# Zero fills moved behind the second pair's loads, and four cross-attention pieces moved within steps 4 and 5, in a one-core decoder layer

## The chip, the cores and the metric

One core of a Trainium2 chip runs the whole kernel as one launch. The metric is the device time of one execution in microseconds (us). The engines are TensorE (PE), VectorE (DVE), ScalarE (ACT), GpSimd (POOL) and SyncE (SP); SP computes nothing here and issues most of the DMAs.

## The reference, cut to what matters

A pre-norm decoder layer for 8 sequences of 100 tokens and width 512: self attention (16 heads, 4 key-value heads, rotary), cross attention to a context of 345 + 16 rows, and a feed-forward part with a shared expert and 60 routed experts, of which each token takes 4. The context's last 16 rows ("DCA") have their own keys, values and softmax.

```python
x = x + attn(layernorm(x))                     # self attention
q = ln(layernorm(x) @ Wq + bq)
ctx     = softmax(q @ k.T * s) @ v             # 345 context rows
ctx_dca = softmax(q @ k_dca.T * s) @ v_dca     # the 16 DCA rows
x = x + (ctx + ctx_dca) @ Wo + bo
x = x + shared(layernorm(x)) + sum_of_top4_experts(layernorm(x))
```

## The kernel before, in words

Each engine has an instruction list of its own, written out by hand, and the lists meet at semaphores. The attention part runs as a loop over 4 pairs of sequences (`i` = 0 to 3; `j` = 0, 1 is the sequence in a pair). Then the routed experts run, two tiles at a time, with the shared expert beside them.

**A pair.** PE begins with the transposes of the normed input (`transpose_x("xT1", 1, j)`), ACT copies them into `xT[j]` (lines 1410 to 1412), and PE projects q, k and v from there (`self_project`). Self attention follows, then the cross attention in steps `t` = 0 to 9. Step `t` takes four of the 32 (sequence, head) combinations: PE computes their scores (`four_scores(t)`), DVE the maxima (`four_max`), ACT the exponentials, PE transposes the previous four (`four_transposes(t - 1, c)`), DVE copies these out (`four_T`), and PE multiplies the ones before with the values (`four_values(t - 2)`). `keep_busy` puts in products of zeros. In the gaps DVE works at the layer norm of the next pair's x, a few instructions at a time (`norm_next`, `few(n)`); it waits for that x (`x_loaded`).

**PSUM.** The eight banks are handed out by a list that `attention_fills` builds from the same hooks that PE's list uses. `HEAD_HOOKS[t]` are PE's extra pieces ahead of a step's transposes, `STEP_HOOKS[t]` those after the first two of them, `TAIL_HOOKS[t]` those after the third. A piece begins only when the earlier user of its bank has been read out. The DCA scores of the second sequence, `("ds", 1)`, and the spread sums of the first, `("rx", 0)`, lie one after the other in bank 7.

**DCA and the sums.** `dca_scores(j)` puts the DCA scores into PSUM; `dca_softmax(j)` on DVE is a generator of three parts: maximum and subtraction (lines 1818 and 1819, which free the bank), sum, reciprocal. `sums(j)` takes the reciprocal of the sums of the main softmax (line 1830) and scales the DCA probabilities (lines 1831 and 1832). ACT spreads the reciprocals over 512 columns (`spread_sums`, `t0`), PE transposes them (`spread_T`, "rx"); from the scaled probabilities PE makes `dca_transpose`, "dpT". In the kernel before, `sums(0)` stands at the end of DVE's step 4, behind the last `few`, and the first part of `dca1` behind it.

**SP's list.** At the start come the weights, then `load_context(1, 0)`, then nine fills of zeros (line 473): 76 tiles of `xs_d` and 36 tiles of `ys_d`, 128 rows of 2 KB each, at most 13 tiles a DMA. Only the scatter and the gather of the routed experts need them. Then, pair by pair: `load_x(i + 1)` (line 433), `load_context(i + 1, 1)` (line 436, once PE has made the values `("vx", 1, 2)` in step 0), and at the pair's end the stores of `xT[0]` into `xT3_d` (line 523), of `xn` and of `xr` (lines 529 and 530). `xT[0]` then holds the transposed input of the gate; ACT overwrites it at the next pair's begin, and for that it waits for the store:

```python
act.wait_ge(xT_stored[0], i * 16 + 1)     # line 1410
x_T("xT1", 0)
x_T("xT1", 1)
```

POOL normalises the heads of the cross attention's keys and queries (`head_norm`, lines 711 to 728), beside DVE's work in steps 1 to 7.

Of the kernel before, what the change touches and what calls it, by code (L numbers as in the profile page):

```python
# [38 lines left out]
TILES = SINGLES + ROUNDS  # L39
assert SINGLES == ROUNDS  # L40
NOV = 36
FILL_STEP = 13
ZERO_FILLS = -(-(TILES + NOV) // FILL_STEP) + -(-NOV // FILL_STEP)
# [39 lines left out]
def attention_fills():  # L83
# [17 lines left out]
    for t in range(STEPS):  # L101
# [4 lines left out]
        if t == 0:  # L106
            out += [(("vx", 1, 2), 7), (("kx", 0, 0), 4), (("xT2", 1), 5)]
        out += [(key, 7) for key in HEAD_HOOKS.get(t, [])]
        parts = [(("xpT", t - 1, c), 4 + (t * LN_ + c) % 2) for c in range(LN_)] if 1 <= t <= FOURS else []
        out += parts[:2] + [(key, 7 if t < 6 else 6) for key in STEP_HOOKS.get(t, [])] + parts[2:]  # L110
        out += TAIL_HOOKS.get(t, [])
# [2 lines left out]

HEAD_HOOKS = {5: [("rx", 0)]}
STEP_HOOKS = {1: [("xq", 1)], 2: [("kx", 0, 1)], 4: [("ds", 1)], 5: [("dpT", 0)], 6: [("xo", 0)], 7: [("vx", 0, 1)]}
TAIL_HOOKS = {3: [(("xqT", 1), 7), (("kx", 0, 2), 4)], 5: [(("vx", 0, 0), 7)], 8: [(("dpT", 1), 3), (("vx", 0, 2), 2)]}
STEP_ZEROS = {1: (0, 0), 2: (0, 2), 3: (3, 0), 4: (0, 2), 5: (2, 0), 6: (0, 2), 7: (0, 2), 8: (2, 0)}  # L120

# [1 line left out]
def decoder_kernel(nc, x, ctxT, dcaT, W_attn, W_out, b_out, Wq, bq, Wkv, bkv, Wdca, bdca, norm, Wo, bo,  # L123
# [6 lines left out]
    with cm:  # L130
# [3 lines left out]
        def sem(name):  # L134
            return cm.enter_context(nc.semaphore(name))
# [6 lines left out]
        xs_d = nc.dram_tensor("xs_d", [(TILES + NOV) * T, D], F32, kind="Internal").ap()  # L142
        ys_d = nc.dram_tensor("ys_d", [(TILES + NOV) * T, D], F32, kind="Internal").ap()
# [72 lines left out]
        vx = [carve(LN_, D) for _ in range(2)]  # L216
# [8 lines left out]
        dpT = [carve(2, S) for _ in range(2)]  # L225
# [87 lines left out]
        pool_pre = sem("pool_preamble")  # L313
# [108 lines left out]
        def wait_drained(eng, i, *key):  # L422

            k = bank_of[key]
            eng.wait_ge(free[k].sem, free[k].at(i, key))
# [3 lines left out]
        def _(sp):  # L429
# [5 lines left out]
            def load_context(i, j):  # L435
                sp.dma_start(c_in[j], ctxT[i * 2 + j, :, :, :]).then_inc(c_loaded[j], 16)
# [29 lines left out]
            sp.wait_ge(first_full, 2 * LN_)  # L466
            load_context(1, 0)

            sp.wait_ge(pool_pre, 7)
            def fill_zeros(rows, first, last):  # L470
                for n in range(first, last, FILL_STEP):
                    m = min(FILL_STEP, last - n)
                    sp.dma_start(rows[n * T:(n + m) * T, :].rearrange("(a p) d -> p a d", p=T),  # L473
                                 zero[0:T, :].rearrange("p (a d) -> p a d", a=1).to_broadcast([T, m, D])).then_inc(zeroed, 16)
                return -(-(last - first) // FILL_STEP)

            fills_started = fill_zeros(xs_d, 0, TILES + NOV)

            fills_started += fill_zeros(ys_d, TILES, TILES + NOV)
            assert fills_started == ZERO_FILLS  # L480

            def load_up(m):
                if m >= 3:
# [11 lines left out]
            for i in range(PAIRS):  # L495
                if i:
                    wait_drained(sp, i, "xT3", 1)
                    store_last_T(i - 1)

                if i:  # L500
                    sp.wait_ge(full[2].sem, full[2].before(i))
                    load_context(min(i + 1, PAIRS - 1), 0)

                sp.wait_ge(x1_ready, i * 2 + 2)
                sp.wait_ge(xr_ready.sem, xr_ready.at(i, (0, 1)))
                load_x(min(i + 1, PAIRS - 1))
                if i + 1 < PAIRS:

                    sp.wait_ge(full[7].sem, full[7].at(i, ("vx", 1, LN_ - 1)))
                    load_context(i + 1, 1)  # L510
                else:

                    sp.wait_ge(full[1].sem, full[1].at(i, ("o", 1)))
                    for j in range(2):
                        sp.wait_ge(xT_stored[j], 16 * i + 1)
                    load_tokens(0, 2 * i, xT3_early)
                    for m in range(3):
                        load_up(m)
                for j in range(2):
                    sp.wait_ge(xn_ready.sem, xn_ready.at(i, (3, j)))  # L520
                    if j == 0:
                        wait_drained(sp, i, "xT3", 0)
                        sp.dma_start(xT3_d[i * 2, :, :], xT[0].rearrange("p a b -> p (a b)")).then_inc(xT_stored[0], 16)
                    elif i == PAIRS - 1:
                        sp.wait_ge(xT_stored[0], 16 * PAIRS + 1)
                        load_tokens(2 * i, 2 * i + 1, xT3_loaded)
                        sp.wait_ge(late_free, 1)
                        store_last_T(i)
                    sp.dma_start(xn3_d[i * 2 + j, :, :], xn[j][0:S, :]).then_inc(xn_stored[j], 16)
                    sp.dma_start(x2_d[i * 2 + j, :, :], xr[j][0:S, :]).then_inc(x2_stored[j], 16)  # L530
# [259 lines left out]
        def _(pe):  # L790
# [30 lines left out]
            with pe.Fori(0, PAIRS) as i:  # L821
# [270 lines left out]
                for t in range(STEPS):  # L1092
# [11 lines left out]
                    if t >= 2:  # L1104
                        four_values(t - 2)
                    for key in HEAD_HOOKS.get(t, []):
                        hooks[key[0]](*key[1:])
                    if 1 <= t <= FOURS:
                        four_transposes(t - 1, 0)
                        four_transposes(t - 1, 1)  # L1110
                    for key in STEP_HOOKS.get(t, []):
                        hooks[key[0]](*key[1:])
# [460 lines left out]
        def _(dve):  # L1573
# [13 lines left out]
            def link(ins):  # L1587

                settle(mark(ins))
# [120 lines left out]
            with dve.Fori(0, PAIRS) as i:  # L1710
# [115 lines left out]
                def sums(j):  # L1826

                    for r in range(4):
                        wait_drained(dve, i, "xs", 4 * j + 3, r)
                    nc.vector.reciprocal(xrec[0:S, j, :], xsum[0:S, j, :]).then_inc(xrec_ready.sem, 1)  # L1830
                    link(nc.vector.tensor_tensor(drec[0:S, j, :], drec[0:S, j, :], xsum[0:S, j, :], ALU.mult))
                    nc.vector.tensor_tensor(dp[j][0:S], dp[j][0:S],
                                            drec[0:S, j, :].rearrange("p (a b) -> p a b", b=1).to_broadcast([S, H, DCA]),
                                            ALU.mult).then_inc(dp_ready.sem, 1)

                def four_max(t, r):
                    j, h = t // 4, 4 * (t % 4) + r
                    k = filled("xs", t, r)
                    nc.vector.tensor_reduce(xnm[0:S, j, h:h + 1], ps[0:S, k, 0:LM], AX, ALU.max, negate=True).then_inc(xmax_ready.sem, 1)  # L1839

                def four_T(t, c):
                    k = filled("xpT", t, c)
                    nc.vector.tensor_copy(xpT[0:LC, c, :], ps[0:LC, k, 0:4 * S]).then_inc(free[k].sem, 1)  # L1843
# [37 lines left out]
                dca0, dca1 = dca_softmax(0), dca_softmax(1)  # L1881
# [18 lines left out]
                def few(n):  # L1900
                    for _ in range(n):
                        next(pieces, None)
                for t in range(1, FOURS + 1):
                    if t == FOURS:
                        sums(1)
                        four_T(t - 1, 0)
                        four_T(t - 1, 2)
                        context_value(0, 2)
                        break
                    four_max(t, 0)  # L1910
                    four_max(t, 1)
                    if t == 6:
                        context_T(0)
                    if t == 7:
                        residual("xo", 0)
                    few(1)
                    four_max(t, 2)
                    four_T(t - 1, 0)
                    four_max(t, 3)
                    if t == 7:  # L1920
                        run(pieces)
                        dve.wait_ge(x1_ready, i * 2 + 4)
                        pieces = norm_x(0)
                    few(2)
                    four_T(t - 1, 1)
                    for key in STEP_HOOKS.get(t, []):
                        if key[0] in ("kx", "vx"):
                            (context_key if key[0] == "kx" else context_value)(*key[1:])
                        elif key[0] == "xq":
                            query(1)  # L1930
                    few(2)
                    four_T(t - 1, 2)
                    for key, _ in TAIL_HOOKS.get(t, []):
                        if key[0] in ("kx", "vx"):
                            (context_key if key[0] == "kx" else context_value)(*key[1:])
                    few(2)
                    if t == 4:
                        sums(0)
                        next(dca1, None)
                    if t in (6, 7):  # L1940
                        next(dca1, None)
                run(pieces)
# [248 lines left out]
```

## Time and profile before

| | us |
|---|---|
| median of 3 runs | 1183.49 |
| lowest, highest | 1182.42, 1189.03 |
| the profiled execution, its own time | 1185.29 |
| span of the profiled execution | 1183.3 |

PE is busy for 1096.6 us of the span (93%), DVE for 505.8, POOL for 371.5, ACT for 263.7. PE's time is the frame: a loss is where PE waits, or where its granted clock is low. Times are counted from the start of the span. A row of a timeline has start, duration, engine, line and tile, and in brackets how long the engine had been idle before it and what ended that. In a table of stretches the last three columns are PE's granted clock (1.00 is 2.4 GHz, 0.50 is 1.2 GHz), the share of the DMA engines and GB/s.

### The profile page before, as it was taken

What the parts mean: (1) busy time and instruction counts of PE and PEld (TensorE: products, weight loads), DVE (VectorE), ACT (ScalarE), POOL (GpSimd) and SP (SyncE); (2) the same over time, 40 slices, a digit from 0 to 9 for tenths busy, and PEclk for the clock granted to TensorE, in tenths of its full rate; (3) what the DMA queues carried; (4) which work ended last, traced back from release to release, by engine and by line L of the source; (5) the groups of instructions that cost most, each with busy time, mean ns of one, the idle gap of its engine ahead of it and who ended that gap; (6) DMA issues with size and microseconds to landing.
All of it is one profiled execution on the core that took longest, in us unless ns stands there. A gap on an engine that the chain in (4) does not pass through costs nothing.

```text
span 1183.3 us, 18962 instructions
## 1 busy us (share of the span) xinstructions
PE 1096.6 (93%) x5550; PEld 592.1 (50%) x5550; DVE 505.8 (43%) x1385; ACT 263.7 (22%) x806; POOL 371.5 (31%) x843
## 2 busy tenths in 40 slices
PE   3999799998999989999999999999999989899797
PEld 1444455445654455544655554555555544444454
DVE  7843574339654395544856701222122211211054
ACT  0332232424332242333414010111111110101000
POOL 2575451855427563474200271000000000000173
PEclk9999899999899999999999999999999998989999
DMA  8999301000010000102004896999999999999744
GB/s 307 325 398 383 114 3 56 15 1 13 2 56 15 13 2 11 46 15 96 1 28 121 306 341 224 384 371 371 379 366 375 368 380 362 376 374 376 252 132 128
DMA packets 76589, 233.17 MB, mean 197 GB/s; under 512 B 11362, under 2 KB 13766, under 8 KB 68814
## 3 DMA queue, kind: packets, MB, share of 16 engines
q1 hardware_dynamic: 58830, 197.90, 46.7%
q10 hardware_dynamic: 11520, 20.98, 5.1%
q0 software_dynamic: 6144, 13.13, 3.6%
q8 instruction: 47, 0.77, 0.3%
q14 instruction: 48, 0.39, 0.1%
HBM read 178.75 MB, written 53.22 MB: 196 GB/s over the span
## 4 chain that ended last, share of the span: by engine, by line
PE 60%; SPq 16%; DVE 10%; DMA 7%; issue 5%; ACT 1%; DVEq 0%; ACTq 0%
PE ps L851 14%; PE ps L935 7%; PE ps L1136 6%; SPq L473 6%; PE ps L1219 5%; PE ps L1320 5%; SPq L546 4%; PE ps L1215 4%; DMA arena<-in_w 3%; DMA arena<-in_se_down 2%; PE ps L1251 2%; PE ps L1247 2%; PE ps L992 2%; PE ps L1193 2%; SPq L551 2%
## 5 line engine op out<-in xcount | busy, mean ns | idle before, releaser
L851 PE MATMUL ps<-arena 128*100 128x512 f32 (+3 forms) x576 | 220.5, 529 | 5.2 <-ACT arena L1342 3.7
L785 POOL DMA_INDIRECT arena<-ys_d,slot_u x32 | 37.5, 1173 | 415.7 <-issue 413.8
L851 PEld LDWEIGHTS ps<-arena 128*100 128x100 f32 (+1 forms) x576 | 87.0, 173 | 100.3 <-issue 90.3
L1219 PE MATMUL ps<-arena 128*64 128x352 f32 x640 | 108.8, 497 | 15.3 <-DMA arena<-in_w 9.0
L2068 DVE COPY arena<-ps 128x512 f32<-128x512 f32 x40 | 27.7, 691 | 221.5 <-PE ps L1207 221.5
L935 PE MATMUL ps<-arena 128*100 128x512 f32 x256 | 114.1, 593 | 0.0
L1136 PE MATMUL ps<-arena 128*128 128x400 f32 x288 | 98.3, 501 | 2.3 <-DVE arena L2048 1.1
L1215 PE MATMUL ps<-arena 128*128 128x352 f32 x320 | 98.1, 459 | 0.8 <-issue 0.8
L1394 ACT ACTIVATE arena<-ps,arena 100x345 f32<-100x345 f32 x128 | 69.4, 546 | 112.4 <-DVE arena L1839 109.8
L1219 PEld LDWEIGHTS ps<-arena 128*64 128x64 f32 x640 | 49.9, 147 | 69.2 <-issue 61.5
L711 POOL TENSOR_TENSOR arena<-arena 115x512 f32<-115x512 f32 (+1 forms) x29 | 30.5, 1052 | 162.2 <-DVE arena L1766 125.0
L1136 PEld LDWEIGHTS ps<-arena 128*128 128x128 f32 x288 | 54.2, 190 | 44.9 <-DVE arena L1810 1.7
L1215 PEld LDWEIGHTS ps<-arena 128*128 128x128 f32 x320 | 59.2, 190 | 30.7 <-issue 1.0
L935 PEld LDWEIGHTS ps<-arena 128*100 128x100 f32 x256 | 42.3, 166 | 62.2 <-issue 58.8
L1508 ACT ACTIVATE arena<-ps 128x352 f32<-128x352 f32 x40 | 18.5, 463 | 223.9 <-PE ps L1219 130.3
L773 POOL DMA_INDIRECT xs_d<-arena,slot_u x32 | 32.6, 1020 | 109.1 <-DVE slot_u L2029 99.6
L1839 DVE TENSOR_REDUCE arena<-ps 100x1 f32<-100x345 f32 x128 | 62.3, 508 | 8.1 <-PE ps L983 7.6
L1320 PE MATMUL ps<-arena 128*128 128x400 f32 x176 | 61.1, 509 | 4.8 <-DMA arena<-in_se_down 4.8
L992 PE MATMUL ps<-ident,arena 100*115 100x100 f32 x384 | 55.4, 284 | 9.8 <-DVE arena L1843 9.1
L992 PEld LDWEIGHTS ps<-ident,arena 100*115 100x115 f32 x384 | 49.2, 193 | 26.3 <-DVE arena L1843 13.1
L1843 DVE COPY arena<-ps 115x400 f32<-115x400 f32 x92 | 52.2, 568 | 21.4 <-PE ps L992 21.3
L1251 PE MATMUL ps<-arena 128*64 128x512 f32 (+1 forms) x240 | 56.0, 600 | 1.0 <-DVE arena L2084 0.9
(227 smaller groups left out, 1522.5 us busy)
## 6 DMA issues: line engine op xcount, KB each, us to landing
arena<-in_w SPq DMA_DIRECT2D x60, 1408.0 KB, 16.8
arena<-in_w SPq DMA_DIRECT2D x60, 512.0 KB, 17.2
xs_d<-zero SPq DMA_DIRECT2D x5, 3328.0 KB, 25.4
arena<-in_w SPq DMA_DIRECT2D x60, 192.0 KB, 19.4
arena<-xs_d ACTq DMA_DIRECT2D x40, 256.0 KB, 8.3
ys_d<-arena ACTq DMA_DIRECT2D x40, 256.0 KB, 8.9
ys_d<-zero SPq DMA_DIRECT2D x2, 3328.0 KB, 25.7
arena<-in_se_up SPq DMA_DIRECT2D x11, 512.0 KB, 6.5
```

What stands on the lines that cost most here:

```text
L473: sp.dma_start(rows[n * T:(n + m) * T, :].rearrange("(a p) d -> p a d", p=T), zero[0:T, :].rearrange("p (a d) -> p a d", a=1).to_broadcast ...
L851: last = nc.tensor.matmul(ps[0:m, k, 0:cols[1] - cols[0]], lhs(c), w[:, c, cols[0]:cols[1]], start=(c == 0), stop=(c == n_c - 1))
L935: last = nc.tensor.matmul(ps[0:S, j, :], cT[c % 2][:, g, :], w_out[:, c * G + g, :], start=(c == 0 and g == 0), stop=(c == KV - 1 and g == ...
L992: last = nc.tensor.transpose(ps[0:LC, k, r * S:(r + 1) * S], xp[(4 * t + r) % NP_][0:S, c * LC:(c + 1) * LC], ident[0:S, 0:S])
L1136: last = nc.tensor.matmul(ps[:, (u % 3) * 2 + gu, 0:400].rearrange("p (a b) -> p a b", a=4), se_w[m % 3][:, c, gu * P:(gu + 1) * P], tok, ...
L1215: last = nc.tensor.matmul(ps[:, 1 + gu, 0:I], xsT[0][:, c, :], w13_s[s][0][:, c, at:at + I], start=(c == 0), stop=(c == DC - 1))
L1219: last = nc.tensor.matmul(ps[half * HALF:(half + 1) * HALF, 3 + gu, 0:I], xsT[1][:, c, half * HALF:(half + 1) * HALF], w13_s[s][1 + half][ ...
L1251: last = nc.tensor.matmul(ps[half * HALF:(half + 1) * HALF, 7, :], hT[1][0:w, n, half * HALF:(half + 1) * HALF], w2_s[s][1 + half][0:w, n, :],
L1320: last = nc.tensor.matmul(ps[:, half * 4 + d, 0:400], w_down[:, m, d * P:(d + 1) * P], hT_all[:, m, half * 400:(half + 1) * 400], start=(m ...
L1394: nc.scalar.activation(xp[(4 * t + r) % NP_][0:S, :], ps[0:S, k, 0:LM], ACT.Exp, bias=xnm[0:S, j, h:h + 1], scale=1.0, accum_out=xsum[0:S, ...
L1839: nc.vector.tensor_reduce(xnm[0:S, j, h:h + 1], ps[0:S, k, 0:LM], AX, ALU.max, negate=True).then_inc(xmax_ready.sem, 1)
L1843: nc.vector.tensor_copy(xpT[0:LC, c, :], ps[0:LC, k, 0:4 * S]).then_inc(free[k].sem, 1)
```

## The change

The nine fills of zeros are issued by SP within the first pair, after `load_x(1)` and `load_context(1, 1)`, and no longer ahead of them. The wait for the tile of zeros moves with them. In steps 4 and 5: PE computes `("ds", 1)` ahead of step 4's transposes and no longer after the first two of them; DVE takes the first part of `dca1` after the fourth maximum of step 4; `sums` is cut in two, the reciprocal (now after the second copy of step 4) and `scale_dca` (for sequence 0 after the second maximum of step 5). Two of the layer-norm pieces of step 4 move behind its third copy. For sequence 1 both halves stay together.

```diff
-HEAD_HOOKS = {5: [("rx", 0)]}
-STEP_HOOKS = {1: [("xq", 1)], 2: [("kx", 0, 1)], 4: [("ds", 1)], 5: [("dpT", 0)], 6: [("xo", 0)], 7: [("vx", 0, 1)]}
+HEAD_HOOKS = {4: [("ds", 1)], 5: [("rx", 0)]}
+STEP_HOOKS = {1: [("xq", 1)], 2: [("kx", 0, 1)], 5: [("dpT", 0)], 6: [("xo", 0)], 7: [("vx", 0, 1)]}
...
             load_context(1, 0)
-            sp.wait_ge(pool_pre, 7)
             def fill_zeros(rows, first, last):
...
-            fills_started = fill_zeros(xs_d, 0, TILES + NOV)
-            fills_started += fill_zeros(ys_d, TILES, TILES + NOV)
-            assert fills_started == ZERO_FILLS
...
                     sp.wait_ge(full[7].sem, full[7].at(i, ("vx", 1, LN_ - 1)))
                     load_context(i + 1, 1)
+                    if i == 0:
+                        sp.wait_ge(pool_pre, 7)
+                        fills_started = fill_zeros(xs_d, 0, TILES + NOV) + fill_zeros(ys_d, TILES, TILES + NOV)
+                        assert fills_started == ZERO_FILLS
...
                     nc.vector.reciprocal(xrec[0:S, j, :], xsum[0:S, j, :]).then_inc(xrec_ready.sem, 1)
+
+                def scale_dca(j):
                     link(nc.vector.tensor_tensor(drec[0:S, j, :], drec[0:S, j, :], xsum[0:S, j, :], ALU.mult))
...
                         sums(1)
+                        scale_dca(1)
...
                     four_max(t, 1)
+                    if t == 5:
+                        scale_dca(0)
...
                     four_max(t, 3)
+                    if t == 4:
+                        next(dca1)
...
                     four_T(t - 1, 1)
+                    if t == 4:
+                        sums(0)
...
-                    few(2)
+                    few(0 if t == 4 else 2)
                     four_T(t - 1, 2)
...
-                    few(2)
-                    if t == 4:
-                        sums(0)
-                        next(dca1, None)
+                    few(4 if t == 4 else 2)
```

## Rows read from the trace of the kernel before

**Rows 1.** Chain of waits, in order of time: start, duration, what.
```profile
102.31 8.78 SPq L473
111.20 17.20 DMA arena<-in_x
```
**Rows 2.** Timeline of SP's queue.
```profile
44.84 41.11 SPq L473 DMA_DIRECT2D xs_d<-zero  x6
...
184.37 0.36 SPq L523 DMA_DIRECT2D xT_d<-arena  x1
...
266.79 0.35 SPq L436 DMA_DIRECT2D arena<-in_ctxT  x1
```
**Rows 3.** Timeline of PE, first pair.
```profile
118.70 0.84 PE L983 MATMUL ps<-arena 32*100 32x345 f32 x8
...
130.08 1.09 PE L992 MATMUL ps<-ident,arena 100*115 100x100 f32 x4 [6.13 <-DVE arena L1843]
...
152.86 0.84 PE L983 MATMUL ps<-arena 32*100 32x345 f32 x8
...
155.84 0.56 PE L1023 MATMUL ps<-ident,arena 100*128 100x100 f32 x4 [1.50 <-DVE arena L1819]
...
161.39 0.84 PE L983 MATMUL ps<-arena 32*100 32x345 f32 x8
...
188.66 0.90 PE L845 MATMUL ps<-ident,arena 100*128 100x100 f32 x8
```
**Rows 4.** Timeline of PE, second pair, and two rows of the fourth.
```profile
269.45 0.84 PE L983 MATMUL ps<-arena 32*100 32x345 f32 x8
...
292.70 0.84 PE L983 MATMUL ps<-arena 32*100 32x345 f32 x8
...
296.86 0.93 PE L1023 MATMUL ps<-ident,arena 100*128 100x100 f32 x4 [2.66 <-DVE arena L1819]
...
305.08 0.84 PE L983 MATMUL ps<-arena 32*100 32x345 f32 x8
...
582.12 0.56 PE L1023 MATMUL ps<-ident,arena 100*128 100x100 f32 x4 [1.07 <-DVE arena L1819]
...
583.61 0.39 PE L957 MATMUL ps<-ident,arena 100*128 100x100 f32 x2
```
**Rows 5.** Stretches: length, PE, PEld, DVE, ACT, POOL busy, clock, DMA, GB/s.
```profile
138.00:140.00 2.00, 2.00 (x9) 1.20 (x8) 0.64 (x2) 0.00 (x0) 1.45 (x8) 0.66 0.00 0
154.00:156.00 2.00, 0.51 (x19) 0.28 (x11) 1.93 (x7) 0.63 (x1) 1.10 (x6) 1.00 0.02 4
303.00:304.00 1.00, 1.00 (x3) 0.37 (x2) 0.00 (x0) 0.00 (x0) 0.91 (x2) 0.91 0.00 0
```
**Rows 6.** The same table, two stretches in which the fills run.
```profile
60.00:70.00 10.00, 9.43 (x72) 5.41 (x71) 5.63 (x16) 2.44 (x7) 9.61 (x13) 1.00 1.05 408
100.00:110.00 10.00, 10.00 (x28) 4.17 (x27) 0.00 (x0) 1.24 (x2) 7.44 (x22) 1.00 1.03 382
```
**Rows 7.** DMA issues: count, KB each, median us to landing.
```profile
ys_d<-zero SPq DMA_DIRECT2D x1, 2560.0 KB, 24.4
...
xT_d<-arena SPq DMA_DIRECT2D x8, 200.0 KB, 1.9
```
**Rows 8.** Timeline of ACT at the second pair's begin.
```profile
189.26 0.90 ACT L1342 ACTIVATE arena<-ps 128x400 f32<-128x400 f32 x2 [3.63 <-PE ps L845]
```
**Rows 9.** Timeline of DVE, second pair, steps 1, 4 and 5.
```profile
267.26 0.55 DVE L1632 TENSOR_SCALAR arena<-arena 100x512 f32<-100x512 f32 x1
...
293.23 1.39 DVE L1632 TENSOR_SCALAR arena<-arena 100x512 f32<-100x512 f32 x1
...
294.71 0.84 DVE L1831 TENSOR_TENSOR arena<-arena 100x16 f32<-100x16 f32 x1
...
296.72 1.35 DVE L1839 TENSOR_REDUCE arena<-ps 100x1 f32<-100x345 f32 x3
```
**Rows 10.** Timeline of POOL in the same stretch.
```profile
294.30 1.22 POOL L711 TENSOR_TENSOR arena<-arena 115x512 f32<-115x512 f32 x1
```

## The prediction

> **What bounds the kernel now.** The frame is the span of the profiled execution, 1183.3 us; its own time is 1185.29, so 2.0 us lie outside the span, and it is 1.8 above the median of 1183.49. Sums below are differences to the profiled execution, and I add them to the median. I read the chain of waits first. In the first pair it runs through SP's queue: the last fill is issued from 102.31 for 8.78 us, then comes the load of the second pair's x, issued at 111.20 and landed 17.20 us later, at 128.40 [rows 1]. The timeline of SP's queue shows why: the fills hold SP from 44.84 on [rows 2], and the x is queued behind them. Next I compared PE in the first pair with PE in the second, where no fill runs. From the scores of step 1 to those of step 5 the first pair takes 152.86 - 118.70 = 34.16 us [rows 3], the second 292.70 - 269.45 = 23.25 [rows 4]: 10.9 us are lost to the late x. Of these 6.13 are a wait of PE, which waits for a copy of DVE while DVE stands at the missing x [rows 3]. The rest is clock: after that wait PE runs at 1.2 GHz, until about 139.3 (0.66 on average over 138 to 140 is 68% of that stretch at half) [rows 5]; half of the 9.3 us from 130.08 is 4.6.
>
> The second place is the wait for DVE line 1819 in step 5, where PE's "rx" wants bank 7, which the DCA scores of sequence 1 hold until that line has run. It costs 1.50 us in the first pair [rows 3], 2.66 in the second and 1.07 in the fourth [rows 4]; the third repeats the second (one pattern, two pairs). After 1.50 the clock was still 1.00 [rows 5]. After 2.66 it was half until about 303.2 (0.91 over 303 to 304) [rows 5], 6.3 us from 296.86, so 3.2 more. That is why step 5 takes 161.39 - 152.86 = 8.53 us in the first pair [rows 3] and 305.08 - 292.70 = 12.38 in the second [rows 4]. Without its wait the first pair's step is 7.0 us of PE work at full clock.
>
> **Part 1, the fills.** Moved up, the x of the second pair lands long before DVE wants it, and the 10.9 us in the first pair go: PE would reach the transposes of the second pair at 188.66 - 10.9 = 177.8 [rows 3], and the store of xT[0] would be wanted at 184.37 - 10.9 = 173.5 [rows 2].
>
> But the fills now stand ahead of that store. They are issued behind `load_context(1, 1)`, which in the second pair ends at 267.14 [rows 2]. The same point of the first pair lies 269.45 - 118.70 = 150.75 earlier [rows 3, 4], at 116.4. They move 112 x 128 x 2 KB = 29.36 MB. The rate beside them falls from 408 to 382 GB/s [rows 6]; at the mean of 395 that is 74.3 us, at the ends 72.0 and 76.9. With 2 us for a first landing (a small store takes 1.9) [rows 7] the last fill lands at 116.4 + 2 + 74.3 = 192.7, between 190.4 and 195.3. The slowest bound is the whole time of before, from the first issue at 44.84 [rows 2] to the last landing at 102.31 + 24.4 = 126.7 [rows 1, 7], 81.9 us with earlier loads still in the queue: 198.3.
>
> Whoever is queued behind is late: the store of line 523, those of lines 529 and 530, then the next pair's context. The row for this is the x of before: issued at 111.20 behind the fills, landed at 128.40 [rows 1], 1.7 us after the last fill. So I take the store to land 1.7 us behind the last fill, at 194.4, and allow 192 to 200. ACT waits for exactly this before it copies the second pair's transposes (line 1410), and PE projects from the copies. ACT's copy starts at 189.26 in the kernel before [rows 8] and at about 194.7 after, with the wait's end: **5.4 us later than before**, although PE is there at 178. The first pair's gain is eaten, whatever it is, and 5.4 more are lost (3 to 11). PE then has waited for about 17 us; waits of 6.13 and 2.66 were followed by 4.6 and 3.2 us lost at half clock (above), so I take 3.9. Part 1 comes to **+9.3** (6 to 15).
>
> The page "DMA: Bandwidth & Descriptors" of the Trainium skill, section "Specifications", gives about 358 GB/s as the limit of HBM per core. By that figure the fills would take 82 us and the sum would be 7.7 us higher. Rows 6, of the same fills, show 382 to 408, so I go by the rows.
>
> **Part 2, steps 4 and 5.** In the first pair it changes nothing that counts, as the pair ends in the wait above. In the second pair I go through it. PE's "ds" ahead of the transposes makes DVE's first copy, and through it PE's third transpose, some 0.3 us late. DVE does lines 1818 and 1819 right after the fourth maximum of step 4, so bank 7 is free some 3.5 us earlier than the 296.86 at which "rx" found it [rows 4], and the reciprocal follows one copy later. PE's "rx" then waits hardly at all (0.2). Next late is "dpT": it wants `scale_dca(0)`, which now follows four pieces of layer norm, two maxima of step 5 and its own two instructions. The third copy of step 4 ends at about 294.4 (293.23, where line 1632 now starts [rows 9], plus 1.2 us of work moved ahead of it). From there: pieces 0.9, maxima 0.9 (1.35 for three, [rows 9]), scaling 0.6 give 296.8 at best. Some of these, from SBUF to SBUF, stretch beside POOL: line 1632 took 1.39 (0.55 in step 1) and line 1831 0.84, as POOL's 512-wide product ran [rows 9, 10]. At worst that is another 1.7 us: 298.5. PE ends step 5's values at 296.86 - 2.66 = 294.2, and from "rx" to "dpT" the fourth pair takes 583.61 - 582.12 = 1.5 [rows 4]; with the 0.3 and the 0.2, PE reaches "dpT" at 296.2. The new wait is 0.6 to 2.3 us; I take 1.6, since that POOL row lies at the same place. Steps 4 and 5 then take 0.3 + 7.0 + 0.2 + 1.6 = 9.1 instead of 12.4: **-3.2 in the second and in the third pair**, if the clock stays. At the bounds that is -4.3 and, with the clock down again, 0. In the fourth pair POOL has no such work left, and 7.0 + 1.07 becomes 7.5 + 0.6: 0.
>
> **Sum.** 5.4 + 3.9 - 3.2 - 3.2 = +2.9: a span of 1186.2, and 1183.5 + 2.9 = 1186.4 for the median. Within +/-5.9 us (0.5%) of before is about what a measurement can't tell from no change.
>
> **The rivals.** *A, slower: the clock falls again.* The new wait for "dpT" reaches the length of the old one. It decides between 1.50 us, which left the clock up [rows 3, 5], and 2.66, which brought it down [rows 4, 5]. Price: both gains of 3.2 go. Time: 1183.5 + 9.3 = 1192.8, with the later landing up to 1198. For it speaks POOL beside DVE, against it that the wait would have to be at its upper bound in both pairs. Chance 0.30.
>
> *B, faster: the store is not held by the fills.* SP would still be issuing until some 66 us after 116.4 (44.84 to 111.1 before) [rows 1, 2], about 179 to 182, but the store would land 2 us later, at 183. ACT's copy would be 6 us early instead of 5.4 late, and with a wait of 5 us the clock still falls: -6 + 3.9 - 6.4 = -8.5, 1175. Against it stands the x of before, which landed behind the fills [rows 1]. The same page of the Trainium skill, section "Queues, rings and completion order", says that completion is not first in, first out per issuing engine, and that a later, smaller transfer can be done earlier; by that rule the time would be this one. No row here shows such an overtaking. Chance 0.10.
>
> *C, faster within the band: no new wait.* Fills at 408 GB/s and hardly a wait for "dpT": 3 + 3.2 - 4.3 - 4.3 = -2.4, 1181. Chance 0.15. That the change doesn't do what it says I exclude for the x, as SP issues it ahead of all fills.
>
> **How the numbers follow.** My forecast, the sum above, has 0.45. Faster by over 0.5% (under 1177.6): B and a little of C, 0.13. Slower by over 0.5% (over 1189.4): nearly all of A and the upper landings of the forecast, 0.36. The rest is 0.51. The range takes C and most of A in and leaves out B and the top of A: 1178 to 1196.
>
> **What would show it.** The x on SP's queue at about 67 us, landed within a few us, and PE at full clock through steps 1 to 4 of the first pair. The fills from 116 to 193; the store of line 523 issued at about 180 and landed near 194; ACT waiting some 16 us ahead of line 1342 at the second pair's begin, then half clock on PE for 6 to 9 us. In step 5 PE's wait moves from "rx" to "dpT", under 2.3 us, with the clock at 1.00. It is wrong if ACT's copy comes ahead of 189, or if step 5 of the second pair stays at 12 us.

## The result, and the profile after

The changed kernel took 1196.59 us (median of four executions, 1189.64 to 1201.43), beside 1182.95 of the kernel before (four, 1181.62 to 1189.03). The ratio is 1.0103, with a 95% interval of 1.0062 to 1.0144: it is slower, by 7 to 17 us. The profiled execution took 1189.64, the shortest of the four, with a span of 1187.9, so the traces below show only 4.6 us more than the span of before. What hides the rest is answered, as far as the traces show it, at the end of the accounting. In the rows of the changed kernel many line numbers are smaller by one or two: L472, L521, L849, L981, L1021 and L1340 are 473, 523, 851, 983, 1023 and 1342 of before. L955 is PE's "dpT", L1355 ACT's copy of "rx" out of PSUM.

The first view is the timeline of SP's queue in the first pair, from 60 us on (columns as in [rows 2]).

```profile
65.90 0.70 SPq L433 DMA_DIRECT2D arena<-in_x  x2
114.77 0.36 SPq L436 DMA_DIRECT2D arena<-in_ctxT  x1
115.17 39.98 SPq L472 DMA_DIRECT2D xs_d<-zero  x6
155.19 25.16 SPq L472 DMA_DIRECT2D ys_d<-zero  x3
180.45 6.88 SPq L521 DMA_DIRECT2D xT_d<-arena  x1
```

The x of the second pair now goes out at 65.90 (before, 111.20 [rows 1]). The fills hold SP from 115.17 to 180.35, and the store of xT[0] comes right behind them. What that store does is in the chain of waits of the same kernel (start, duration, what), and in ACT's timeline:

```profile
180.45 17.52 DMA xT_d<-arena
...
198.07 0.51 ACT arena L1340
```

```profile
198.07 0.90 ACT L1340 ACTIVATE arena<-ps 128x400 f32<-128x400 f32 x2 [23.97 <-DMA xT_d<-arena]
```

The store of 200 KB takes 17.52 us to land; in before it took 1.9 at the median [rows 7]. ACT is idle for 23.97 us, and the bracket names the store as what ended it. Its copy starts at 198.07; the same copy of before started at 189.26 [rows 8]: 8.8 us later, although nothing in the first pair waits for x any more.

The table of stretches (columns as in [rows 5]) shows what runs in that wait. The second row is the end of the fills, the third the first products after the wait.

```profile
180.00:190.00 10.00, 0.90 (x8) 0.72 (x8) 1.51 (x7) 0.00 (x0) 0.00 (x0) 0.62 1.04 383
194.00:196.00 2.00, 0.00 (x0) 0.00 (x0) 0.00 (x0) 0.00 (x0) 0.00 (x0) 0.50 0.79 183
...
202.00:204.00 2.00, 2.00 (x5) 0.79 (x4) 0.00 (x0) 0.00 (x0) 0.00 (x0) 0.79 0.00 0
```

The other engines do little (first row) and then nothing at all, while the DMA engines are full with zeros. The last fill is issued at 171.3 and lands 24.1 us later, at 195.4; the store lands at 197.97.

PE's timeline (as in [rows 3, 4]): steps 1, 5 and 6 of the first pair, the begin of the second pair, steps 4 to 6 of the second pair, and two rows behind the fourth pair.

```profile
117.43 0.84 PE L981 MATMUL ps<-arena 32*100 32x345 f32 x8
...
141.08 0.84 PE L981 MATMUL ps<-arena 32*100 32x345 f32 x8
...
145.96 0.39 PE L955 MATMUL ps<-ident,arena 100*128 100x100 f32 x2 [1.90 <-ACT arena L1355]
...
150.01 0.84 PE L981 MATMUL ps<-arena 32*100 32x345 f32 x8
...
198.71 10.03 PE L849 MATMUL ps<-arena 128*100 128x512 f32 x24 [17.44 <-ACT arena L1340]
...
299.25 0.84 PE L981 MATMUL ps<-arena 32*100 32x345 f32 x8
...
303.97 0.84 PE L981 MATMUL ps<-arena 32*100 32x345 f32 x8
...
305.58 0.56 PE L1021 MATMUL ps<-ident,arena 100*128 100x100 f32 x4
...
308.84 0.59 PE L955 MATMUL ps<-ident,arena 100*128 100x100 f32 x2 [1.90 <-ACT arena L1355]
...
314.41 0.84 PE L981 MATMUL ps<-arena 32*100 32x345 f32 x8
...
618.46 6.08 PE L849 MATMUL ps<-arena 128*100 128x61 f32 x16 [0.59 <-ACT arena L1340]
...
633.21 21.76 PE L1134 MATMUL ps<-arena 128*128 128x400 f32 x64 [0.31 <-ACT lg_late L1461]
```

The last row is the point at which I compare kernels from here on: 64 products of the shared expert, the first long stretch of PE behind the four pairs. The rows of before that belong to it:

```profile
189.89 7.98 PE L851 MATMUL ps<-arena 128*100 128x512 f32 x24 [0.33 <-ACT arena L1342]
...
288.39 0.84 PE L983 MATMUL ps<-arena 32*100 32x345 f32 x8
...
610.47 4.38 PE L851 MATMUL ps<-arena 128*100 128x61 f32 x16 [0.59 <-ACT arena L1342]
...
623.53 21.76 PE L1136 MATMUL ps<-arena 128*128 128x400 f32 x64 [0.31 <-ACT lg_late L1463]
```

The point lies at 623.53 there, so the four pairs cost 9.7 us more. The account, each line as the shift of a point against before:

| point | before | after | shift | step of it |
|---|---|---|---|---|
| ACT's copy, second pair | 189.26 | 198.07 | +8.8 | +8.8 the store behind the fills |
| step 4, second pair | 288.39 | 299.25 | +10.9 | +2.1 half clock after the wait |
| step 6, second pair | 305.08 | 314.41 | +9.3 | -1.5 steps 4 and 5 |
| step 6, third pair | 448.53 | 456.52 | +8.0 | -1.3 steps 4 and 5 |
| step 6, fourth pair | 587.66 | 595.63 | +8.0 | 0 |
| the 64 products | 623.53 | 633.21 | +9.7 | +1.7 products of line 849, 6.08 instead of 4.38 us |

Behind that point lie the routed experts, which the change doesn't touch. From the first load of an expert's weights to the load of w_down they took 427.6 us in the trace of before and 422.0 in this one: 5.6 us less, which hides half of the loss. Over the ten traces of this study the stretch took between 422.0 and 433.4, whatever the kernel. So the profiled execution shows +4.6 where the four pairs alone would give +9.7. The two medians are 13.6 us apart; no trace shows the longer executions of this run, so what they add to the 9.7 is not shown.

### The profile page after: what moved, and what is told of

It reads as the page before. It is cut to its first block, busy times and chain, and to the rows that moved or that the text cites. A ratio compares the mean times of both kernels' runs of the same rounds, so it can differ in the third digit from the quotient of the medians.

```text
span 1187.9 us, 18962 instructions
## 1 busy us (share of the span) xinstructions
PE 1091.5 (92%) x5550; PEld 586.8 (49%) x5550; DVE 504.8 (42%) x1385; ACT 263.9 (22%) x806; POOL 370.3 (31%) x843
## 4 chain that ended last, share of the span: by engine, by line
PE 72%; DVE 12%; DMA 6%; issue 5%; SPq 3%; ACT 1%; DVEq 0%; ACTq 0%
PE ps L849 16%; PE ps L933 9%; PE ps L1217 7%; PE ps L1134 6%; PE ps L1213 6%; PE ps L1318 5%; PE ps L1249 3%; PE ps L1245 3%; DMA arena<-in_se_down 2%; DMA arena<-in_w 2%; PE ps L922 2%; PE ps L1191 2%; PE ps L990 2%; DMA xT_d<-arena 1%; SPq L544 1%
## 5 line engine op out<-in xcount | busy, mean ns | idle before, releaser
L849 PE MATMUL ps<-arena 128*100 128x512 f32 (+3 forms) x576 | 222.8, 534 | 21.7 <-ACT arena L1340 20.8
L849 PEld LDWEIGHTS ps<-arena 128*100 128x100 f32 (+1 forms) x576 | 87.6, 174 | 118.5 <-issue 109.0
L990 PE MATMUL ps<-ident,arena 100*115 100x100 f32 x384 | 51.9, 271 | 3.7 <-DVE arena L1843 3.2
L990 PEld LDWEIGHTS ps<-ident,arena 100*115 100x115 f32 x384 | 45.9, 181 | 19.0 <-issue 11.8
```

The source lines that it names most:

```text
L849: last = nc.tensor.matmul(ps[0:m, k, 0:cols[1] - cols[0]], lhs(c), w[:, c, cols[0]:cols[1]], start=(c == 0), stop=(c == n_c - 1))
L990: last = nc.tensor.transpose(ps[0:LC, k, r * S:(r + 1) * S], xp[(4 * t + r) % NP_][0:S, c * LC:(c + 1) * LC], ident[0:S, 0:S])
```

## The experiments

Two questions were open: is it the queue that made the store late, and what did the new order of steps 4 and 5 give, as the clock fell there again. The kernels ran in two groups, each beside the kernel before on the same chip: 1184.14 us (19 executions) for the first four, 1185.1 (17) for the others. "Point" is the start of the 64 products, 623.53 in before.

| kernel | median us (n) | ratio, interval | ACT's copy | point |
|---|---|---|---|---|
| fills moved only | 1192.7 (5) | 1.0082, 1.0059 to 1.0105 | 199.89 | 633.94 |
| steps 4 and 5 only | 1181.58 (10) | 0.9979, 0.995 to 1.0008 | 185.80 | 620.63 |
| fills right behind x | 1173.41 (4) | 0.9908, 0.988 to 0.9936 | 180.64 | 612.35 |
| store on ACT's queue | 1177.77 (10) | 0.9955, 0.9937 to 0.9973 | 181.50 | 616.19 |
| the changed kernel again | 1195.89 (10) | 1.0087, 1.0054 to 1.012 | 198.57 | 634.58 |
| fills right behind x, again | 1173.77 (6) | 0.9891, 0.9833 to 0.9948 | 178.98 | 613.98 |
| the same, fewer pieces | 1164.7 (6) | 0.9825, 0.9781 to 0.9869 | 178.69 | 606.86 |
| the same, ACT's copy first | 1168.14 (6) | 0.9866, 0.9822 to 0.9911 | 178.80 | 607.48 |

**The fills alone.** The new place of the fills, with steps 4 and 5 as before.

```diff
-            fills_started = fill_zeros(xs_d, 0, TILES + NOV)
...
                     load_context(i + 1, 1)
+                    if i == 0:
+                        sp.wait_ge(pool_pre, 7)
+                        fills_started = fill_zeros(xs_d, 0, TILES + NOV) + fill_zeros(ys_d, TILES, TILES + NOV)
```

> The fills alone are moved behind load_context(1, 1); steps 4 and 5 are as before. Theory Q (the fills hold the store of xT[0] in SP's queue, and ACT's first copy of the second pair waits for it): that copy starts near 198 as in the changed kernel (198.07), against 189.26 before; PE pays some 2 us of half clock behind it; the steps' gain of about 3.5 is missing, so the 64 products of line 1136 start at about 623.5 + 10.8 = 634, 11 us later than before, and the time is about 1194 to 1199. Rival S (what cost is the steps' part, and the fills' new place pays): the time is at or under 1183 and the copy starts ahead of 189.

The point moved by +10.4 us, as expected; the median, 1192.7, lies a little under the expected range. ACT's timeline has the wait for the store:

```profile
199.89 0.90 ACT L1340 ACTIVATE arena<-ps 128x400 f32<-128x400 f32 x2 [21.27 <-DMA xT_d<-arena]
```

Part 1 by itself accounts for the whole loss. The stretch of the routed experts was at its longest here (first row; before in the second), which is the difference between a span of 1200.0 and what the point would have given:

```profile
666.00:1099.00 433.00, 408.64 (x1745) 212.31 (x1745) 95.95 (x241) 46.74 (x89) 32.65 (x32) 0.97 0.99 356
```
```profile
655.00:1083.00 428.00, 409.36 (x1755) 213.03 (x1753) 96.39 (x244) 46.69 (x89) 32.65 (x32) 0.98 0.99 360
```

In both the DMA engines are full (0.99) and PE waits a little more when less arrives: 356 GB/s against 360, and 364 in the trace of after. What sets that rate from one execution to the next was not tested.

**Steps 4 and 5 alone.** The fills ahead of x as before, with the new order of the steps.

```diff
             load_context(1, 0)
+            sp.wait_ge(pool_pre, 7)
+            fills_started = fill_zeros(xs_d, 0, TILES + NOV) + fill_zeros(ys_d, TILES, TILES + NOV)
```

> Steps 4 and 5 as in the changed kernel, the fills back ahead of the first pair. Theory Q: the first pair is as before (PE's wait of 6.1 us for the late x), step 5 of the second and the third pair takes about 10.5 us instead of 12.3 with a wait of 1.9 us for ACT's copy of rx; the shared expert's 64 products start at 620 to 621 instead of 623.5, the time is about 1180. Rival S: it is slower than before by 5 us or more.

The point came 2.9 us earlier, the time within what can be told from none. PE's timeline has the wait for x again, and the new wait in step 5:

```profile
128.49 0.86 PE L990 MATMUL ps<-ident,arena 100*115 100x100 f32 x4 [5.13 <-DVE arena L1843]
...
294.48 0.39 PE L955 MATMUL ps<-ident,arena 100*128 100x100 f32 x2 [1.91 <-ACT arena L1355]
295.80 3.50 PE L849 MATMUL ps<-arena 128*115 128x512 f32 x4
```

The first pair gives 3.5 us (ACT's copy at 185.80 instead of 189.26), but not by the new order: its step 4 already begins 3.7 us earlier than in before (144.59 instead of 148.26). The fills went out 1.1 us earlier in this execution (43.74 instead of 44.84), and PE's wait for the late x is 1.0 us shorter. The rest of the four pairs loses 0.6: steps 4 and 5 win 1.3 us in the second pair and 1.3 in the third, and the products of line 849 behind the second and the fourth pair lose 1.5 and 1.7 (6.05 and 6.08 us instead of 4.38). So this trace shows no gain by the new order over all four pairs. The four products behind the wait take 3.50 us, where the kernel with fewer pieces (below), at a clock of 1.00, takes 1.91: a wait of 1.91 us, and half clock after it.

**The fills right behind x.** Still behind the x, but no longer behind the second context, which is wanted late.

```diff
                 load_x(min(i + 1, PAIRS - 1))
+                if i == 0:
+                    sp.wait_ge(pool_pre, 7)
+                    fills_started = fill_zeros(xs_d, 0, TILES + NOV) + fill_zeros(ys_d, TILES, TILES + NOV)
...
                     load_context(i + 1, 1)
-                    if i == 0:
-                        sp.wait_ge(pool_pre, 7)
-                        fills_started = fill_zeros(xs_d, 0, TILES + NOV) + fill_zeros(ys_d, TILES, TILES + NOV)
```

> The changed kernel, with the nine fills one place earlier in SP's list: right behind load_x(1), ahead of the wait for the values and load_context(1, 1). Theory Q: they run from about 67 to 148, so neither the x (landed near 69) nor the store of xT[0] (wanted at about 173) is held; load_context(1, 1) lands near 149 and is wanted at about 188. The first pair loses its 10.9 us wait and the second starts on time: ACT's first copy near 178, the 64 products at 623.5 - 10.9 - 3 = 609 to 611, the time about 1169 to 1172, faster than both kernels. Rival N (whatever runs beside the fills is slowed by them, wherever they stand): part of the gain is missing, 1176 or more.

SP's timeline, and ACT's row:

```profile
66.68 0.70 SPq L433 DMA_DIRECT2D arena<-in_x  x2
67.42 39.16 SPq L472 DMA_DIRECT2D xs_d<-zero  x6
106.63 25.93 SPq L472 DMA_DIRECT2D ys_d<-zero  x3
...
175.40 0.34 SPq L521 DMA_DIRECT2D xT_d<-arena  x1
```
```profile
180.64 0.90 ACT L1340 ACTIVATE arena<-ps 128x400 f32<-128x400 f32 x2 [3.98 <-PE ps L843]
```

The same nine fills, 48 us earlier, are over before the store is wanted: the last lands at about 148, the store is issued at 175.40, and ACT's copy waits for PE. The copy, the point (612.35) and the median came 1 to 3 us later than expected. The point is still 11.2 us ahead of before and 20.9 ahead of the changed kernel.

**The store on another queue.** The fills stay where the change put them; only the store of xT[0] goes from SP's queue to ACT's.

```diff
-                        sp.dma_start(xT3_d[i * 2, :, :], xT[0].rearrange("p a b -> p (a b)")).then_inc(xT_stored[0], 16)
...
+                wait_drained(act, i, "xT3", 0)
+                act.dma_start(xT3_d[bass.ds(i * 2, 1), :, :].rearrange("a p n -> (a p) n"),
+                              xT[0].rearrange("p a b -> p (a b)")).then_inc(xT_stored[0], 16)
```

> The changed kernel with one DMA on another queue: ACT, not SP, issues the store of xT[0] at each pair's end (line 521). The fills stay where the change puts them. Theory Q (order in one queue): the store in the first pair is issued near 174 and lands within about 6 us, with the fills still running; ACT's first copy of the second pair starts at 178 to 182 and the time is about 1170 to 1178. Rival N (the DMA engines are full, so any store is late until the fills are through): it lands near 196 as in the changed kernel, and the time stays at 1190 or more.

ACT's timeline, SP's, and the DMA issues from 170 to 185 us:

```profile
173.34 0.40 ACTq L1456 DMA_DIRECT2D xT_d<-arena  x1
...
181.50 0.90 ACT L1339 ACTIVATE arena<-ps 128x400 f32<-128x400 f32 x2 [6.99 <-PE ps L842]
```
```profile
155.68 25.65 SPq L472 DMA_DIRECT2D ys_d<-zero  x3
181.43 6.34 SPq L526 DMA_DIRECT2D xn_d<-arena  x1
```
```profile
xT_d<-arena ACTq DMA_DIRECT2D x1, 200.0 KB, 7.9
```

The store lands in 7.9 us, at about 181.2, beside the fills. From ACT's queue the same store takes 3.5 us in each of the other pairs, so the fills beside it cost it 4.4 us. From SP's queue it landed at 197.97, 16.7 us later. The rival that any store is late until the fills are through falls. ACT's copy now waits for PE, and not all of that is PE's work: its transposes there begin 3.29 us after the products ahead of them, and the trace names nothing that PE waits for. The changed kernel and the fills alone have the same gap (3.17 and 3.26), the fills right behind x 0.27. What it is was not looked for. The Trainium skill, page "DMA: Bandwidth & Descriptors", section "Queues, rings and completion order", has each DMA engine take turns between the queues that have work for it. This trace agrees: the store from ACT's queue landed in 7.9 us, while SP was still issuing fills.

**The changed kernel and the fills right behind x, once more.** No edit; they ran beside the next two on the same chip.

> The changed kernel once more, for a second trace and more times: its first four times spread from 1189.6 to 1201.4. Theory E (the attention part's loss is fixed, about 8 to 10 us at the start of the 64 products, and the rest of the spread lies in the routed experts, whose time from the first expert's load to the load of w_down is set by the weights' DMAs): the 64 products start at 631 to 634 again and the ratio comes to about 1.008. Rival (the attention part itself varies by 5 us or more): they start outside of 630 to 636.

> e3_fills_behind_x beside e5 and e6 on one chip, as the step they are compared with. Theory E: the 64 products start at 610 to 613, the ratio is 0.989 to 0.992.

Both ratios repeat: 1.0087 after 1.0103, and 0.9891 after 0.9908. ACT's copy at 198.57 and the point at 634.58 show the same loss, with a routed stretch of 425.5 us instead of 422.0. Both points lie 1.4 and 1.6 us behind those of the first traces, 0.6 and 1.0 past what was expected; the rival, a point outside of 630 to 636, falls.

**Fewer pieces ahead of the scaling.** In the changed kernel DVE does four pieces of layer norm behind the third copy of step 4. This kernel has the fills right behind x, and takes those pieces out of step 4; they follow later.

```diff
-                    few(4 if t == 4 else 2)
+                    few(0 if t == 4 else 2)
```

> e3_fills_behind_x, with none of the layer-norm pieces behind step 4's third copy (they run in step 5's own places). Theory D (the 1.9 us for which PE waits at dpT in the second and the third pair come from DVE: the pieces, stretched beside POOL, lie ahead of the two maxima, and ACT's first exponential of step 5, its copy of rx and the scaling all follow these): the wait falls to 0.5 us or less in all pairs, step 5 of the second and the third pair from about 10.5 to about 8 us, the clock stays up there, and the shared expert's 64 products start at about 608 instead of 612.35. Time about 1168 to 1170. Rival B (the order in bank 7: dpT has to wait for ACT's copy of rx, which stands behind an exponential): more than 1 us of the wait stays.

DVE's timeline of the changed kernel shows what stands ahead of PE's row at 308.84: two pieces stretched beside POOL (0.91 and 1.04 us), then the maxima, then the scaling. ACT's exponential can start only at the maxima's end, and its copy of "rx" out of bank 7, which PE's next transposes need, stands behind that.

```profile
305.31 0.91 DVE L1613 SCALAR_TENSOR_TENSOR arena<-arena 100x1 f32<-100x1 f32 x1
306.26 1.04 DVE L1630 TENSOR_SCALAR arena<-arena 100x512 f32<-100x512 f32 x1
307.22 0.93 DVE L1839 TENSOR_REDUCE arena<-ps 100x1 f32<-100x345 f32 x2
308.07 0.16 DVE L1831 TENSOR_TENSOR arena<-arena 100x16 f32<-100x16 f32 x1
308.26 0.42 DVE L1832 TENSOR_TENSOR arena<-arena 100x256 f32<-100x256 f32 x1
```
```profile
307.76 0.55 ACT L1392 ACTIVATE arena<-ps,arena 100x345 f32<-100x345 f32 x1 [2.30 <-DVE arena L1839]
...
308.30 0.49 ACT L1355 ACTIVATE arena<-ps 128x400 f32<-128x400 f32 x1
```

POOL's timeline of the same stretch, and DVE's of the fourth pair, where POOL does nothing from 586 to 592 us:

```profile
305.17 1.04 POOL L709 TENSOR_TENSOR arena<-arena 115x512 f32<-115x512 f32 x1
306.29 2.09 POOL L712 TENSOR_TENSOR arena<-arena 115x256 f32<-115x256 f32 x4
```
```profile
589.28 0.16 DVE L1613 SCALAR_TENSOR_TENSOR arena<-arena 100x1 f32<-100x1 f32 x1
589.48 0.55 DVE L1630 TENSOR_SCALAR arena<-arena 100x512 f32<-100x512 f32 x1
```

The same two pieces are 1.24 us shorter there, and PE's wait at "dpT" is 1.25 us shorter: 0.65 instead of 1.90. So the stretching accounts for two thirds of the wait.

Without the pieces PE's timeline of the same step 5, and the stretch it lies in, read:

```profile
282.54 0.84 PE L981 MATMUL ps<-arena 32*100 32x345 f32 x8
...
285.41 0.39 PE L955 MATMUL ps<-ident,arena 100*128 100x100 f32 x2
...
290.04 0.84 PE L981 MATMUL ps<-arena 32*100 32x345 f32 x8
```
```profile
282.00:290.00 8.00, 7.65 (x70) 5.14 (x68) 7.42 (x19) 4.00 (x13) 6.31 (x17) 1.00 0.01 3
```

No wait ahead of line 955, the clock at 1.00, and a step of 290.04 - 282.54 = 7.50 us where the changed kernel needs 10.44. The point is 7.1 us ahead of the same kernel with the pieces; at 1164.7 us, 0.9825 of before, this is the fastest version of the study, faster than both kernels of this case. The rival that bank 7's order keeps more than 1 us of the wait falls.

**ACT's copy ahead of the exponential.** The last kernel, and also ACT's copy of "rx" ahead of the exponential.

```diff
-                        four_exp(t, r)
                         if (t, r) == (5, 0):
                             spread(0)
+                        four_exp(t, r)
```

> e5_fewer_pieces, with ACT's copy of rx of sequence 0 ahead of the first exponential of step 5 and no longer behind it. Theory D: no further change beyond 0.5 us a pair, as the scaling on DVE comes last anyway (64 products within 2 us of e5). Rival B: only now the wait at dpT falls under 0.5 us, and the 64 products start 4 us or more earlier than in e5.

Nothing more came of it: the point is 0.6 us behind that of the kernel before it, and the time, 0.9866, lies in an overlapping interval. Once the pieces are gone, the order on ACT doesn't matter. Whether that order alone would have helped with the pieces in place was not tried.

## Why the prediction was right or wrong

The prediction named 1186.4 us, and a change within 0.5% as likeliest; the kernel became slower by about 1.0%, which had the second chance. 1183.49 x 1.0103 is 1195.7, at the upper edge of the range. That the time lies in the range is in part luck: what happened is rival A, the clock falling again, with less than its price of 3.2 us a pair, and with a loss behind the fourth pair that no sum had. The mechanism of part 1 was right. Against the sum of +2.9 the landing came out 3.4 us higher, the half clock 1.8 lower and the steps 3.6 higher, and 1.7 were not in it: 2.9 + 3.4 - 1.8 + 3.6 + 1.7 = 9.8, the measured +9.7.

**Right: where the gain goes.** The wait for x is gone, and the first pair gets 10.5 of its 10.9 us: from the scores of step 1 to those of step 5 it takes 141.08 - 117.43 = 23.65 us instead of 34.16 [rows 3]. The fills then hold the store, ACT waits for the store and PE for ACT, 17.44 us where about 17 were expected. That these two agree is luck, as PE's transposes came later than predicted too (180.37 instead of 177.8), by nearly as much as ACT's copy (198.07 instead of 194.7). The experiment with ACT's queue shows the queue as the cause.

**Mis-sized: the landing, +8.8 instead of +5.4.** The begin was predicted for 116.4 and came at 115.17. The fills took 80.2 us instead of 76.3, first issue to last landing, and the store landed 2.6 behind them instead of 1.7. The two stretches taken for the rate [rows 6] both lie in the middle. In the middle the rate held here too (383 GB/s), but it was 183 from 194 to 196 us, as the fills end. Over the whole it is 29.36 MB / 80.2 us = 366 GB/s. My slowest bound, from before's own begin and end, gave 81.9 us, and it was the nearer one: a time from first issue to last landing is better than a rate out of the middle. The Trainium skill, page "DMA: Bandwidth & Descriptors", section "Specifications", gives about 358 GB/s per core as the limit of HBM. The trace does not bear it out as a limit here: in the middle the fills ran above it, at 383, and only their slower begin (345 from 115 to 125 us) and end bring the whole near it. The estimate of 82 us by that figure came close, but not for that figure's reason.

**Mis-sized: the half clock after it, +2.1 instead of +3.9.** PE came back at 198.71 with the clock at 0.50, and the 0.79 over 202 to 204 puts its rise at about 202.8: 4.1 us at half, so 2.1 lost, and the 24 products of the first projections took 10.03 us instead of the 7.98 of before. The waits of 6.13 and 2.66 us in the trace of before were followed by 9.3 and 6.3 us at half, and I took their mean cost. The longest wait cost least. The work behind it differs (here 24 products of 512 columns, there mostly shorter ones); whether that is the reason was not tried.

**Mis-sized: steps 4 and 5, 1.5 + 1.3 instead of 3.2 + 3.2.** This is the term that carries the sign. The old wait at "rx" went, as predicted, and a new one came at "dpT", 1.90 us, predicted as 0.6 to 2.3 with 1.6 as the value. Its size was nearly met. What failed is the condition "if the clock stays". The first pair of the changed kernel shows what that condition is worth: its wait at "dpT" was 1.90 us too, the clock stayed up, and step 5 took 150.01 - 141.08 = 8.93 us. In the second and the third pair it took 10.44 and 10.59. With 8.93, steps 4 and 5 would have gained 3.0 us in each, near the predicted 3.2 (12.38 - 9.1 is 3.3); the fall took 1.5 and 1.7 of that back.

Rival A put the point of decision between 1.50 and 2.66, and I wrote against it that the wait would have to be at its upper bound, 2.3. Of 17 waits of 1.89 to 1.91 us at this place, in the traces of six runs, 12 were followed by half clock and 5 were not: one fall of five in the first pair, 11 of 12 in the second and the third. In the third pair of the changed kernel the wait ended at 450.81, with the clock at 1.00 over 450 to 452, and it fell only after that:

```profile
452.00:454.00 2.00, 2.00 (x6) 0.93 (x6) 1.03 (x2) 0.66 (x3) 1.51 (x7) 0.51 0.04 8
```

So the length of the wait alone doesn't decide, and no single value could have been right for it. For the two pairs in the sum the larger part of the chance belonged on "down"; what sets them apart from the first was not tried. The fourth pair, with a wait of 0.65 us, kept its clock, and gained 0 as predicted. How much of the 1.5 and 1.3 belongs to the new order stays open: in the kernel with the fills alone the old step 5, with its wait of 2.68 us, took 10.99 and 11.34 us in these pairs, where the kernel before took 12.38 and 12.30 for the same instructions.

**Wrong: who releases "dpT".** I named the scaling. The trace names ACT's copy of "rx" out of bank 7, behind the exponential, behind the maxima of DVE. I had counted bank 7 as free once "rx" could start, and had not asked who hands it on from "rx". The scaling ended at 308.68, the copy at 308.79: two chains of equal length, both behind the same four pieces. The reason that I gave for the wait's size, pieces stretched beside POOL, was therefore still the right one for two thirds of it (1.24 of 1.90 us), and taking the pieces out ended both chains.

**Not in the sum: 1.7 us behind the fourth pair.** The 16 products of line 849 took 6.08 us instead of 4.38, at half clock, after the same wait of 0.59 us. They took 6.0 to 6.1 in seven of the eight traces with the new steps and 4.38 in the kernel with the store on ACT's queue, in the kernel before and in the one with the fills alone. The same products took 6.05 to 6.08 us behind an earlier pair too in four of these eight traces, and in no pair of the two traces with the old steps. Something ahead of that place in the new order seems to matter; what it is stays open.

**Not in the sum: the routed experts.** Their stretch moves by up to 11 us from one execution to another, with the DMA engines busy for 0.99 of it in all ten traces, and 1185.29 of before was one execution of these. A single trace can't show this.

**Rival B fell.** The store didn't overtake the fills. The rule of the Trainium skill on which B rested (page "DMA: Bandwidth & Descriptors", section "Queues, rings and completion order": completion is not first in, first out per issuing engine) allows an overtaking and doesn't promise one; what the section names is a later DMA on one DMA engine beside an earlier one on sixteen. In the traces here the x or the store that SP issued behind the fills landed behind them.

## What to carry to other kernels

A bulk transfer that is moved on an in-order queue takes its delay along: list what is queued behind the new place and when each of these is wanted, and look for a gap longer than the transfer's whole time, from first issue to last landing (here 67 to 148 us fits, 115 to 195 doesn't); or give the small urgent transfer a queue of its own. When an operation is moved ahead to free a buffer, follow the buffer through its next holder too, and look for small work that stands ahead of both on the engine that releases it. A predicted wait near the length at which the clock is seen to fall can cost nearly its own length again (here 1.5 to 1.7 us behind 1.90); make it clearly short, or count the loss.

## What the runs showed of the hardware that was not expected

- Waits of PE of the same length, 1.89 to 1.91 us, at the same place of the same work were followed by half clock 12 times in 17: once in five in the first pair, 11 times in 12 in the second and the third.
- Two small pieces on DVE took 0.91 and 1.04 us beside POOL's products, and 0.16 and 0.55 with POOL idle.
- A store of 200 KB beside fills that keep the DMA engines full landed in 7.9 us from another queue, and in 17.52 us from the queue of the fills, issued 7.1 us later.
- The rate of the fills is 383 GB/s in the middle and 183 in the last two microseconds.
- The same routed stretch took from 422.0 to 433.4 us, at 356 to 364 GB/s with the DMA engines busy for 0.99 of it.
